# Graph and attention layer on one Trainium2 core: the clearing of a table's unused columns moved to a later stage, and half of a block's normalisation moved to ScalarE

## The chip, the cores and the metric

The kernel runs on one core of a Trainium2 chip. The metric is the device time of one execution in microseconds (us). The core has five engines that work side by side and wait for each other by semaphores: TensorE (PE, with its weight loads PEld), VectorE (DVE), ScalarE (ACT), GpSimd (POOL) and SyncE (SP). SP only issues DMA transfers in this kernel; POOL issues the indirect ones (gathers and scatters by a list of row numbers).

## The reference, cut to what matters

A graph layer and linear attention share a normalised input; a second graph layer (attention over edges) then mixes four experts.

```python
x: (12500, 256)   src, dst: (200000,), dst sorted
xn = layernorm(x)
h  = batchnorm(xn @ w1.T + b1); h = relu(h) @ w2.T + b2; xw = h @ w_gcn.T
gcn = segment_sum(xw[src] * norm[:, None], dst) + b_gcn        # self loops included
mix = linear_attention(xn)                                     # wq, wk, wv, wo
x = x + gcn + mix
hf = layernorm(x) @ W_gat; a_src, a_dst per head               # one row of 24 numbers per node
x = x + experts(layernorm(x), gates from attention over 131072 edges and self loops)
```

## The kernel before, in words

The 12,500 nodes are 25 blocks (NB) of 500, a block is four tiles (SUB) of 125 nodes. The stages follow one another, each a program block of its own:

- `first_half` (0 to 261 us): SP loads block k of x into one of three buffers (`load`, through `rows_in_two`, L163). DVE takes statistics (L615 to L620), ACT takes the root (L566), DVE inverts it (L625) and normalises the block's four tiles (L630). PE transposes (`turn`, L520), ACT copies the transposes out of PSUM (L592), PE multiplies by w1 (`project`, L530), ACT adds the bias (L603), DVE takes statistics of the result (L636). Beside it DVE counts the edge list's sections by `outside` (L643) and chooses rows (L649), POOL gathers these rows (L508) and ACT counts in them (`inside`, L574). SP stores the transposed block (L487).
- `table_rows` (271 to 400 us) writes the gather table to DRAM.
- `gather_mix` (400 to 2746 us): POOL gathers table rows, 128 rows of 1 KB in each of 1664 indirect DMAs, four to a group, in a ring of four groups (L1039). DVE builds a one-hot matrix for each group (L1377), PE multiplies (L1109), DVE adds the products to a sum that stays in SBUF (L1394). Other work is dealt out over the 832 slots of this loop (two gathers each): the attention, a sort of the second edge list and, from slot HIST = 547 on, the degrees of the second list. For the degrees SP loads that list once more (`raw_d`, L1097) and DVE waits for it in `numbers(0)`, slot 544 (L1472, L1473).
- `second_norm` fills the first 24 columns of the second table `gtab` (12,500 rows of 128 numbers, TWIDE; 24 used, TROW), whose other 104 columns have been cleared by one DMA from a zeroed tile: 12,500 pieces of 416 bytes. `gat_experts` gathers whole rows of `gtab`. Then `gat_finish` and `finale`.

Every engine runs its instructions in the order in which they are written. SP's DMAs all go through one hardware queue (q1 in the profile), POOL's through another (q0). In slot p of the gather loop PE runs `gathered(p)` and DVE `build` (even slots) and `add(p)`. Three limits tie them:

```python
pool.wait_ge(mm_s, 2 * (g - RING + 1))   # POOL, group g: the products of group g-4 are done
pe.wait_ge(add_s, 2 * p - 6)             # PE, slot p: the sums of slot p-4 are done
dve.wait_ge(raw_s, 16)                   # DVE, numbers(0): raw_d has landed
```

In `first_half` ACT's order for block k is: root(k+1), copies of block k, `inside(k-3)`, bias of block k. DVE's is: statistics(k+1), outside(k), inverse and normalise(k+1), choose(k), statistics of the product of block k-1.

Of the kernel before, what the change touches and what calls it, by code (L numbers as in the profile page):

```python
# [16 lines left out]
P = 128  # L17
# [368 lines left out]
def first_half(nc, K, A):  # L386
# [7 lines left out]
    with ExitStack() as ctx:  # L394
# [20 lines left out]
        st6 = m.sb("a_st6", [P, 2, SUB, 6])  # L415
        mv = m.sb("a_mv", [P, 2, SUB, 2])
        rs = m.sb("a_rs", [P, 2, SUB, 2])
        stats = m.sb("a_stats", [P, KC, NB, 6])
        node = m.sb("a_node", [P, NT])
        minus = m.sb("a_minus", [P, NT])  # L420
# [5 lines left out]
        diff = m.sb("a_diff", [P, 2, TN])  # L426
        deg = m.sb("a_deg", [P, NT])
        degree = m.sb("a_degree", [P, NT])
        blank = m.sb("a_blank", [P, TWIDE - TROW])
        tail = m.sb("tail", [P, 2], I32)  # L430
        after = m.sb("after", [P, 1], I32)
        fall = m.sb("fall", [P, 2])
# [3 lines left out]
        ph = m.ps("a_ph", [P, KC, 512])  # L436
        pw = m.ps("a_pw", [P, 512])
        pb = m.ps("a_pb", [P, 512])
        (w_s, both_s, bias_s, st_s, mv_s, eps_s, root_s, rec_s, xn_s, turned, xnT_s, h_s, hT_s, stat_s, deg_s, v,
         blank_s) = (m.sem("a_" + s) for s in (  # L440
             "w", "both", "bias", "st", "mv", "eps", "root", "rec", "xn", "turned", "xnT", "h", "hT", "stat", "deg", "v",
             "blank"))
        (dst_s, src_s, after_s, short_s, rows_out, pay_s, pairs_out, pad_s, edge_s, fell, spread_s, head_s, met_s, row_s, side_s,
         node_s, diff_s) = (m.sem("e_" + s) for s in (
             "dst", "src", "after", "short", "rows_out", "pay", "pairs_out", "pad", "edge", "fell", "spread", "head", "met", "row",
# [10 lines left out]
        with nc.Block() as block:  # L456
            @block.sync
            def _(sp):
                def load(k):
                    if k >= 3:  # L460
                        sp.wait_ge(xn_s, (k - 2) * SUB)
                    rows_in_two(sp, xin[:, k % 3], A.x[k * BN:(k + 1) * BN].rearrange("(j p) f -> p j f", p=TN), x_in[k % 3])

                by_part = A.dst.rearrange("(p c) -> p c", p=c)
                rows_in_two(sp, raw[:, 1], by_part, dst_s)
                load(0)
                for t, a in ((w1T, A.w1T), (w2, A.w2), (wgT, A.wgT)):
                    sp.dma_start(t[:], a.rearrange("(c p) o -> p c o", p=P)).then_inc(w_s, 16)
                with nc.allow_non_contiguous_dma(reason="biases"):
                    for t, a in ((b1c, A.b1), (b2c, A.b2)):  # L470
                        sp.dma_start(t[:], a.rearrange("(c p) -> p c", p=P)).then_inc(w_s, 16)
                with nc.allow_non_contiguous_dma(reason="one value per partition"):
                    sp.dma_start(after[0:c - 1], by_part[1:c, 0:1]).then_inc(after_s, 16)
                sp.wait_ge(short_s, 1)
                rows_in_two(sp, K.gcn_dst.rearrange("(p i) h -> p (i h)", p=c), short, rows_out)
                load(1)
                load(2)
                rows_in_two(sp, raw[:, 0], A.src.rearrange("(p c) -> p c", p=c), src_s)

                sp.wait_ge(blank_s, 1)  # L480
                sp.dma_start(K.gtab.rearrange("(t p) f -> p t f", p=TN)[:, :, TROW:TWIDE],
                             blank[q].unsqueeze(1).to_broadcast([TN, NT, TWIDE - TROW])).then_inc(blank_s, 16)
                for k in range(NB):
                    if k + 3 < NB:
                        load(k + 3)
                    sp.wait_ge(xnT_s, (k + 1) * KC)
                    sp.dma_start(K.xnT_d[k], xnT[:, k % 2]).then_inc(stored[k % 2], 16)  # L487
                    if k == 3:
                        sp.wait_ge(pay_s, 2)
                        rows_in_two(sp, K.gcn_pairs[0:E_GCN].rearrange("(p c) a -> p c a", p=c), K.gcn_pay, pairs_out)  # L490
                        sp.wait_ge(pad_s, 2)
                        sp.dma_start(K.gcn_pairs[E_GCN:E_GCN + P], tail[:]).then_inc(pairs_out, 16)
                for s in range(2):
                    sp.wait_ge(stored[s], 16 * ((NB + 1 - s) // 2))
                sp.wait_ge(blank_s, 17)
                sp.wait_ge(pairs_out, 48)

            @block.gpsimd
# [13 lines left out]
            @block.tensor  # L512
            def _(pe):
                def turn(k):
                    pe.wait_ge(xn_s, (k + 1) * SUB)
                    if k:
                        pe.wait_ge(xnT_s, k * KC)
                    for ch in range(KC):
                        for j in range(SUB):
                            mm = pe.transpose(ptr[:, ch, j * TN:(j + 1) * TN], xn[q, k % 2, j, ch * P:(ch + 1) * P],  # L520
                                              K.ident[q, q])
                        mm.then_inc(turned, 1)
# [39 lines left out]
            @block.scalar  # L562
            def _(act):
                def root(k):
                    act.wait_ge(eps_s, k + 1)
                    act.activation(rs[q, k % 2, :, 1], rs[q, k % 2, :, 0], ACT.Sqrt).then_inc(root_s, 1)  # L566

                def inside(g):
                    act.wait_ge(got[g % DEEP], 64 * (g // DEEP + 1))
                    if g:  # L570
                        act.wait_ge(side_s, 4 * g)
                    for j in range(4):
                        t = 4 * g + j
                        act.activation(seen[z, j], rows[z, g % DEEP, j], ACT.Sign, bias=minus[z, t:t + 1],  # L574
                                       accum_out=side[z, t:t + 1]).then_inc(side_s, 1)

                def paired(a):
                    act.wait_ge((src_s, dst_s)[a], 32)
                    act.copy(K.gcn_pay[0:c, :, a], raw[0:c, a]).then_inc(pay_s, 1)

                root(0)
                act.wait_ge(w_s, 16 * 5)
                act.wait_ge(node_s, 4)
                for k in range(NB):
                    if k + 1 < NB:
                        root(k + 1)
                    if k >= 2:
                        act.wait_ge(stored[k % 2], 16 * (k // 2))
                        act.wait_ge(h_s, (k - 1) * KC)
                    for ch in range(KC):  # L590
                        act.wait_ge(turned, k * KC + ch + 1)
                        act.copy(xnT[:, k % 2, ch], ptr[:, ch, 0:BN]).then_inc(xnT_s, 1)  # L592
                    if k in (1, 2):
                        paired(2 - k)
                    if k >= 3:
                        inside(k - 3)
                    if k == 20:
                        act.wait_ge(pay_s, 2)
                        act.wait_ge(edge_s, 7)
                        act.wait_ge(rows_out, 32)  # L600
                    for o in range(KC):
                        act.wait_ge(h_s, k * KC + o + 1)
                        act.activation(hT(k)[:, o], ph[:, o, 0:BN], ACT.Identity, bias=b1c[:, o:o + 1]).then_inc(hT_s, 1)  # L603
                for g in range(NB - 3, NB):
                    inside(g)
                act.wait_ge(deg_s, 1)
                act.activation(deg[q], deg[q], ACT.Sqrt).then_inc(root_s, 1)

            @block.vector
            def _(dve):  # L610
# [11 lines left out]
                def normalise(k):  # L622
                    s = k % 2
                    dve.wait_ge(root_s, k + 1)
                    dve.reciprocal(rs[q, s, :, 0], rs[q, s, :, 1]).then_inc(rec_s, 1)  # L625
                    dve.wait_ge(rec_s, k + 1)
                    if k >= 2:
                        dve.wait_ge(turned, (k - 1) * KC)
                    for j in range(SUB):
                        dve.tensor_scalar(xn[q, s, j], xin[q, k % 3, j], mv[q, s, j, 0:1], rs[q, s, j, 0:1],  # L630
                                          ALU.subtract, ALU.mult).then_inc(xn_s, 1)

# [34 lines left out]
                        dve.wait_ge(fell, 2)  # L667
                        dve.tensor_scalar(K.unsorted[:], pb[0:1, 0:1], 1.0, None, ALU.min).then_inc(edge_s, 1)

                dve.memset(blank[:], 0.0).then_inc(blank_s, 1)  # L670
                dve.tensor_scalar(node[:], K.iota[:, 0:NT], float(TN), K.part[:], ALU.mult, ALU.add).then_inc(node_s, 1)
                dve.tensor_tensor(diff[:, 0], K.ident[:, 1:POST], K.ident[:, 0:TN], ALU.subtract).then_inc(diff_s, 1)
                dve.wait_ge(node_s, 1)
# [252 lines left out]
def gather_mix(nc, K, A):  # L926
# [10 lines left out]
    with ExitStack() as ctx:  # L937
# [46 lines left out]
        heads = m.sb("m_heads", [P, KC, P])  # L984
        rn = m.sb("m_rn", [P, 2, SUB, 8])
        cnt2, upto, ends, tot = (m.sb("m_" + s, [P, NT]) for s in ("cnt2", "upto", "ends", "tot"))
        pa = m.ps("m_pa", [P, 512])
        pb = m.ps("m_pb", [P, 512])
        pc = m.ps("m_pc", [P, 512])
# [40 lines left out]
        with nc.Block() as block:  # L1030
# [14 lines left out]
            def _(sp):  # L1045
# [48 lines left out]
                        load2(k + 2)  # L1094
                for s in range(2):
                    sp.wait_ge(out_x[s], 32 * ((NB + 1 - s) // 2))
                sp.dma_start(raw_d, A.edge_index[1].rearrange("(p c) -> p c", p=P)).then_inc(raw_s, 16)  # L1097

            @block.tensor
            def _(pe):  # L1100
# [271 lines left out]
            def _(dve):  # L1372
# [241 lines left out]
                dve.tensor_scalar(bq[:, 1], bq[:, 0], -1.0, None, ALU.mult).then_inc(one_s, 1)  # L1614
                dve.tensor_tensor(b_out[0:1, 0], b_out[0:1, 0], b_out[0:1, 1], ALU.add).then_inc(one_s, 1)
                dve.memset(K.gat_last[:], 0).then_inc(one_s, 1)
                for p in range(SLOTS):
                    if p % 2 == 0:
                        tiles = tiles_of(p // 2)
# [932 lines left out]
```

## Time and profile before

| | us |
|---|---|
| median of 3 runs | 4793.2 (4790.67 to 4804.6) |
| the profiled execution | 4790.88 |
| its span in the trace | 4789.0 |
| PE busy | 3688.3 (77%) |
| POOL busy | 3085.5 (64%) |
| DVE busy | 2604.3 (54%) |
| ACT busy | 880.5 (18%) |

The shares are means over stages with different limits, so each stage is read for itself. The trace's times count from the start of the span. In a timeline a row is a start, a duration (of a whole run of equal instructions where xN stands at the end), an engine, a line of the kernel and the tiles; the bracket is the idle time of that engine before it and what ended it. SPq is the time that SP's issue of a DMA took, not that of its transfer. "issue" in the bracket is the engine's own time between instructions.

### The profile page before, as it was taken

Reading aid. Unit: us, or ns where it says so; the run is one execution under the profiler, and the core shown is the slowest. Engines: PE = TensorE matmul, PEld = TensorE weight load, DVE = VectorE, ACT = ScalarE, POOL = GpSimd, SP = SyncE. Lnnn points to the kernel's source line nnn. Section 1 sums busy time; section 2 is a strip of 40 time slices with the busy share of each in tenths; the row PEclk is TensorE's granted clock in tenths of the full one; section 3 lists DMA queues with packets and bytes.
Section 4 is the critical chain, followed back from the end, with each engine's and each line's share of the span. In section 5 each row is a group of like instructions: output and inputs, shape, how many; then the busy total and the mean of one; then the engine's idle time right before and its main releaser. Section 6 shows DMA issues by size and latency. Waiting matters only on the chain. (4 is left out here: it accounts for less than half of the span.)

```text
span 4789.0 us, 44151 instructions
## 1 busy us (share of the span) xinstructions
PE 3688.3 (77%) x13162; PEld 2442.9 (51%) x13162; DVE 2604.3 (54%) x6218; ACT 880.5 (18%) x1738; POOL 3085.5 (64%) x3019
## 2 busy tenths in 40 slices
PE   3667888888798998787887564799999999700377
PEld 1355555455555555555555354466666666500255
DVE  5946776666666556666666364134334333312476
ACT  2653222222100000000000011222222223200232
POOL 2515777777776776777777500777777777777630
PEclk7989999999887998777677655899999999955689
DMA  6645444444454664333333765444444334322588
GB/s 178 188 98 152 129 130 132 130 130 130 125 154 132 182 177 131 89 91 89 92 91 89 71 193 137 132 114 113 138 115 113 117 106 138 97 63 63 114 209 196
DMA packets 262492, 606.63 MB, mean 127 GB/s; under 512 B 88254, under 2 KB 144369, under 8 KB 256893
## 3 DMA queue, kind: packets, MB, share of 16 engines
q0 software_dynamic: 124496, 304.94, 24.1%
q1 hardware_dynamic: 137772, 299.02, 22.2%
q8 instruction: 103, 1.69, 0.1%
q14 instruction: 121, 0.99, 0.1%
HBM read 447.85 MB, written 155.88 MB: 126 GB/s over the span
## 5 line engine op out<-in xcount | busy, mean ns | idle before, releaser
L1039 POOL DMA_INDIRECT g_rows<-table,gcn_srcT x1664 | 1758.2, 1057 | 568.0 <-issue 485.7
L1109 PE MATMUL g_ps<-g_rows,g_hot 128*125 128x256 f32 x3328 | 1064.3, 456 | 337.4 <-issue 229.6
L1902 POOL DMA_INDIRECT n_rows<-gtab,so_own x1122 | 1095.6, 977 | 341.9 <-issue 341.9
L1394 DVE TENSOR_TENSOR acc<-acc,g_ps 125x256 f32 x1664 | 696.4, 419 | 691.6 <-PE g_ps L1109 565.6
L1109 PEld LDWEIGHTS g_ps<-g_rows,g_hot 128*125 128x125 f32 x3328 | 685.8, 223 | 622.8 <-issue 410.0
L1842 PE MATMUL p_ph<-f_xfT,f_w 128*128 128x500 f32 x1344 | 576.7, 585 | 64.2 <-DMA f_xfT<-xfT_d 64.2
L1848 PE MATMUL p_py<-f_w,f_hh 128*125 128x256 f32 x2688 | 590.4, 379 | 0.0
L1848 PEld LDWEIGHTS p_py<-f_w,f_hh 128*125 128x125 f32 x2688 | 504.5, 188 | 101.1 <-issue 27.4
L2045 DVE TENSOR_TENSOR p_ob<-p_py,p_xb 125x512 f32<-125x512 f32 x168 | 115.6, 691 | 699.0 <-PE p_py L1848 698.6
L1842 PEld LDWEIGHTS p_ph<-f_xfT,f_w 128*128 128x128 f32 x1344 | 256.4, 191 | 348.6 <-issue 343.5
L2073 ACT ACTIVATE f_hh<-p_ph,f_b 128x500 f32<-128x500 f32 x336 | 221.4, 677 | 616.4 <-PE p_ph L1842 616.1
L1377 DVE TENSOR_TENSOR g_hot<-iota,gcn_dstT 128x500 f32<-128x500 f32 x416 | 281.2, 676 | 27.6 <-issue 16.9
L1199 PE MATMUL m_pa<-m_area 128*100 128x125 bf16 x1024 | 276.5, 405 | 0.0
L2125 PE MATMUL f_pt<-ident,gat_tail 128*20 128x128 f32 x3 | 0.8, 402 | 285.1 <-PEq L84 285.1
L1199 PEld LDWEIGHTS m_pa<-m_area 128*100 128x100 bf16 x1024 | 170.5, 167 | 86.1 <-issue 29.8
L1129 PE MATMUL m_pb<-m_area 128*125 128x512 f32 x400 | 197.4, 616 | 19.0 <-DVE m_area L1404 18.8
L508 POOL DMA_INDIRECT so_x<-gcn_dst,a_row x100 | 100.6, 1006 | 147.2 <-DVE a_row L649 124.0
L530 PE MATMUL a_ph<-a_xnT,w1T 128*128 128x500 f32 x200 | 105.8, 679 | 102.1 <-ACT a_xnT L592 102.1
L1895 POOL DMA_INDIRECT n_first<-gtab,gat_head x1 | 0.9, 943 | 278.1 <-POOLq L84 278.1
L1842 PE MATMUL z_ph<-f_xfT,f_w 128*128 128x500 f32 x256 | 118.2, 619 | 67.6 <-ACT f_hh L2321 54.2
L1790 ACT ACT_TABLE_LOAD x1 | 1.3, 1283 | 881.0 <-PEq L84 881.0
L2125 PEld LDWEIGHTS f_pt<-ident,gat_tail 128*20 128x20 f32 x3 | 0.3, 107 | 285.6 <-issue 285.5
(338 smaller groups left out, 4329.8 us busy)
## 6 DMA issues: line engine op xcount, KB each, us to landing
o_d<-p_ob SPq DMA_DIRECT2D x21, 1920.0 KB
z_ob<-o_d SPq DMA_DIRECT2D x21, 1920.0 KB
g_rows<-table,gcn_srcT POOLq DMA_INDIRECT x1664, 3.0
n_rows<-gtab,so_own POOLq DMA_INDIRECT x1122
gout<-n_o SPq DMA_DIRECT2D x33, 408.0 KB, 2.5
xnT_d<-a_xnT SPq DMA_DIRECT2D x25, 500.0 KB
m_area<-xnT_d SPq DMA_DIRECT2D x25, 500.0 KB, 3.8
qT_d<-m_area SPq DMA_DIRECT2D x25, 500.0 KB, 3.1
```

The costliest lines, as they stand in the source:

```text
L530: mm = pe.matmul(ph[:, o, 0:BN], w1T[:, ch, o * P:(o + 1) * P], xnT[:, k % 2, ch], start=ch == 0, stop=ch == KC - 1)
L1039: pool.indirect_dma_start(out=rows[:, g % RING, j], out_offset=None, in_=K.table, in_offset=bass.IndirectOffsetOnAxis(ap=K.gcn_srcT[:, 4 * ...
L1109: mm = pe.matmul(ps[q, p % 4, b], hot[:, g % 4, 2 * j + b], rows[:, g % RING, 2 * j + b], start=True, stop=True, skip_group_check=True)
L1129: pe.matmul(pb[q], xnT[:, k % 2, c, j * TN:(j + 1) * TN], wkv[:, c].rearrange("p a o -> p (a o)"), start=c == 0, stop=False, skip_group_ch ...
L1199: mm = pe.matmul(pa[0:NT, q], ot[:, r % 2, b], on[:, r % 2, :, b], start=r == 0 and b == 0, stop=r == half - 1 and b == HB - 1)
L1377: dve.tensor_tensor(hot[:, g % 4], K.iota[:, q].unsqueeze(1).to_broadcast(shape), K.gcn_dstT[:, 4 * g:4 * g + 4].unsqueeze(2).to_broadcast ...
L1394: dve.tensor_tensor(a, a, ps[q, p % 4, b], ALU.add).then_inc(add_s, 1)
L1842: mm = pe.matmul(ph[:, o, 0:BN], self.w1[:, e, c, o * P:(o + 1) * P], self.xfT[:, s, c], start=c == 0, stop=c == KC - 1)
L1848: mm = pe.matmul(py[0:TN, e % 2, j // 2, (j % 2) * D:(j % 2 + 1) * D], self.hh[:, e % 2, c, j * TN:(j + 1) * TN], self.w2[:, e, c], start= ...
L1902: pool.indirect_dma_start(out=rows[:, c % 3, j], out_offset=None, in_=K.gtab, in_offset=bass.IndirectOffsetOnAxis(ap=K.gat_src[:, c * W + ...
L2045: dve.tensor_tensor(ob[0:TN, s, pair, e], py[0:TN, e % 2, a].rearrange("p (j f) -> p j f", j=2), xb[0:TN, pair], ALU.add).then_inc(ob_s, 1)
L2073: act.activation(X.hh[:, e % 2, o], ph[:, o, 0:BN], ACT.Gelu, bias=X.b1[:, e, o:o + 1]).then_inc(hh_s, 1)
```

## The change

1. The 104 unused columns of `gtab` are no longer cleared in `first_half`. The zeroed tile, its semaphore, the memset and the DMA move to `gather_mix`. There the DMA is issued by SP after the last stores of the attention's result, directly ahead of the load of `raw_d`.
2. In `first_half` DVE normalises two of a block's four tiles, ACT the other two, as `rs * x + off`. DVE computes `off = -mean * rs` in one more small instruction. ACT's part stands right behind root(k+1), ahead of the copies of block k. SP's reload of a buffer and PE's transposes wait for both halves.

```diff
-                sp.wait_ge(blank_s, 1)
-                sp.dma_start(K.gtab.rearrange("(t p) f -> p t f", p=TN)[:, :, TROW:TWIDE],
-                             blank[q].unsqueeze(1).to_broadcast([TN, NT, TWIDE - TROW])).then_inc(blank_s, 16)
                 for k in range(NB):
                     if k + 3 < NB:
                         load(k + 3)
...
+                def normalise(k):
+                    s = k % 2
+                    act.wait_ge(off_s, k + 1)
+                    if k >= 2:
+                        act.wait_ge(turned, (k - 1) * KC)
+                    for j in range(SUB // 2, SUB):
+                        act.activation(xn[q, s, j], xin[q, k % 3, j], ACT.Identity, bias=off[q, s, j:j + 1],
+                                       scale=rs[q, s, j, 0:1]).then_inc(xna_s, 1)
...
                     if k + 1 < NB:
                         root(k + 1)
+                        normalise(k + 1)
...
                     dve.wait_ge(rec_s, k + 1)
+                    dve.scalar_tensor_tensor(off[q, s], mv[q, s, :, 0], -1.0, rs[q, s, :, 0], ALU.mult, ALU.mult
+                                             ).then_inc(off_s, 1)
                     if k >= 2:
                         dve.wait_ge(turned, (k - 1) * KC)
-                    for j in range(SUB):
+                    for j in range(SUB // 2):
...
                 for s in range(2):
                     sp.wait_ge(out_x[s], 32 * ((NB + 1 - s) // 2))
+                sp.wait_ge(blank_s, 1)
+                sp.dma_start(K.gtab.rearrange("(t p) f -> p t f", p=TN)[:, :, TROW:TWIDE],
+                             blank[q].unsqueeze(1).to_broadcast([TN, NT, TWIDE - TROW])).then_inc(blank_s, 16)
                 sp.dma_start(raw_d, A.edge_index[1].rearrange("(p c) -> p c", p=P)).then_inc(raw_s, 16)
+                sp.wait_ge(blank_s, 17)
```

SP's order of DMAs at the start of `first_half`, before (`a_xin` is a buffer for x; the load behind the clearing is that of block 3; `acc<-in_src` is the source list):

```order
L163 DMA acc<-in_src 120x1600
L163 DMA acc<-in_src 5x1600
L481 DMA gtab<-a_blank 125x100x104
L163 DMA a_xin<-in_x 120x4x256
L163 DMA a_xin<-in_x 5x4x256
L487 DMA xnT_d<-a_xnT 128x1000
```

In the change the row of L481 is gone from here, and block 3's load follows the source list. SP's order at the end of its work in `gather_mix`, now (`m_area<-in_edge_index` is the load of `raw_d`; before, it followed the stores of `pre_d` directly):

```order
L163 DMA pre_d<-m_area 120x1024
L163 DMA pre_d<-m_area 5x1024
L1108 DMA gtab<-m_blank 125x100x104
L1110 DMA m_area<-in_edge_index 128x1024
L1040 UNCONDITIONAL_BRANCH
```

The clearing now stands between the last stores and the load that DVE waits for. ACT's order for one block in `first_half`, now (`a_rs` root, `a_xn` normalise, `a_xnT` copies, `so_own` inside, `acc` bias):

```order
L562 ACTIVATE a_rs<-a_rs 125x4
L570 ACTIVATE a_xn<-a_xin,a_off,a_rs 125x256 x2
L599 COPY a_xnT<-a_ptr 128x500 x2
L579 ACTIVATE so_own,a_side<-so_x,a_minus 126x400 x4
L610 ACTIVATE acc<-a_ph,b1c 128x500 x2
```

The row of L570 is new; the other four stood in this order before.

## Rows read from the trace of the kernel before

**Rows 1.** Timeline of SP, first stage: start, duration of the issue, DMA.

```profile
15.20 0.34 SPq L481 DMA_DIRECT2D gtab<-a_blank  x1
16.38 60.49 SPq L163 DMA_DIRECT2D a_xin<-in_x  x2
```

**Rows 2.** Timeline of DVE around its longest wait in the first stage.

```profile
35.76 0.16 DVE L663 TENSOR_TENSOR fall<-fall 128x1 f32<-128x1 f32 x1
81.09 1.40 DVE L615 BATCH_NORM_STATS2 a_st<-a_xin 125x6 f32<-125x256 f32 x4 [45.17 <-DMA a_xin<-in_x]
```

**Rows 3.** Windows: busy PE, PEld, DVE, ACT, POOL; last PE clock, DMA share, GB/s.

```profile
30.00:40.00 10.00, 4.48 (x16) 2.36 (x16) 5.78 (x15) 3.19 (x4) 5.21 (x6) 0.91 0.53 148
50.00:60.00 10.00, 0.00 (x0) 0.00 (x0) 0.00 (x0) 0.00 (x0) 0.00 (x0) 0.50 0.38 98
```

**Rows 4.** Timeline of the first blocks: DVE's second and third inverse, PE's first product.

```profile
22.03 6.49 PE L530 MATMUL a_ph<-a_xnT,w1T 128*128 128x500 f32 x8 [3.70 <-ACT a_xnT L592]
...
23.16 0.18 DVE L625 RECIPROCAL a_rs<-a_rs 125x4 f32<-125x4 f32 x1
...
31.04 0.17 DVE L625 RECIPROCAL a_rs<-a_rs 125x4 f32<-125x4 f32 x1
```

**Rows 5.** Timeline of one later block of the first stage, DVE, ACT and PE.

```profile
132.30 1.39 DVE L615 BATCH_NORM_STATS2 a_st<-a_xin 125x6 f32<-125x256 f32 x4
...
134.47 1.03 ACT L592 COPY a_xnT<-a_ptr 128x500 f32<-128x500 f32 x2
...
135.56 3.62 PE L530 MATMUL a_ph<-a_xnT,w1T 128*128 128x500 f32 x8 [2.84 <-ACT a_xnT L592]
...
136.88 0.16 DVE L625 RECIPROCAL a_rs<-a_rs 125x4 f32<-125x4 f32 x1
...
137.07 1.38 DVE L630 TENSOR_SCALAR a_xn<-a_xin,a_mv,a_rs 125x256 f32<-125x256 f32 x4
...
139.22 0.68 ACT L603 ACTIVATE acc<-a_ph,b1c 128x500 f32<-128x500 f32 x1 [0.70 <-PE a_ph L530]
139.62 1.39 DVE L615 BATCH_NORM_STATS2 a_st<-a_xin 125x6 f32<-125x256 f32 x4
...
141.67 0.21 ACT L566 ACTIVATE a_rs<-a_rs 125x4 f32<-125x4 f32 x1 [1.78 <-DVE a_rs L620]
```

**Rows 6.** Groups by line and form: busy us, mean ns of one.

```profile
L630 DVE TENSOR_SCALAR a_xn<-a_xin,a_mv,a_rs 125x256 f32<-125x256 f32 x100 | 34.5, 409 | 0.9
L835 ACT ACTIVATE acc<-r_tmp,dinv 125x256 f32<-125x256 f32 x100 | 44.7, 497 | 33.2 <-DVE r_tmp L911 33.2
L828 ACT ACTIVATE r_r<-acc,r_shift,r_scale 128x500 f32<-128x500 f32 x50 | 37.0, 789 | 3.4 <-DVE r_shift L854 3.4
```

**Rows 7.** PE: first and last of six long products, the next; a window inside.

```profile
98.94 5.32 PE L530 MATMUL a_ph<-a_xnT,w1T 128*128 128x500 f32 x8 [2.25 <-ACT a_xnT L592]
...
208.67 5.31 PE L530 MATMUL a_ph<-a_xnT,w1T 128*128 128x500 f32 x8 [2.84 <-ACT a_xnT L592]
...
215.99 3.62 PE L530 MATMUL a_ph<-a_xnT,w1T 128*128 128x500 f32 x8 [1.14 <-ACT a_xnT L592]
...
208.00:211.00 3.00, 2.33 (x3) 1.11 (x4) 2.96 (x12) 3.00 (x10) 1.24 (x2) 0.63 0.67 237
```

**Rows 8.** The load of raw_d: SP's timeline, and issue to landing by line.

```profile
1887.25 0.36 SPq L1097 DMA_DIRECT2D m_area<-in_edge_index  x1
DMA to landing us min/median/max: 4.0/4.0/4.0
```

**Rows 9.** DVE's timeline at slot 544; POOL's group of gathers up to 1894.0 us.

```profile
1895.91 0.90 DVE L1473 TENSOR_SCALAR m_area<-m_area 128x1024 int32<-128x1024 int32 x1
L1039 POOL DMA_INDIRECT g_rows<-table,gcn_srcT x1096 | 1111.1, 1014 | 390.2 <-issue 317.2 <-PE g_ps L1109 72.9
```

**Rows 10.** POOL's waits from 1895 to 2660 us: us in total, times, longest.

```profile
POOL g_rows L1039 <- PE g_ps L1109: 3.4, 11, 0.3
```

**Rows 11.** Window of the gather loop shortly before the load, columns as in rows 3.

```profile
1860.00:1880.00 20.00, 18.28 (x80) 11.83 (x79) 11.55 (x26) 0.56 (x1) 15.26 (x16) 1.00 0.43 131
```

More of the change, by code:

```diff
@@ L417, in first_half @@
         rs = m.sb("a_rs", [P, 2, SUB, 2])
+        off = m.sb("a_off", [P, 2, SUB])
         stats = m.sb("a_stats", [P, KC, NB, 6])
@@ L428, in first_half @@
         degree = m.sb("a_degree", [P, NT])
-        blank = m.sb("a_blank", [P, TWIDE - TROW])
         tail = m.sb("tail", [P, 2], I32)
@@ L438, in first_half @@
         pb = m.ps("a_pb", [P, 512])
[L439 to L442, printed above, removed]
+        (w_s, both_s, bias_s, off_s, xna_s, st_s, mv_s, eps_s, root_s, rec_s, xn_s, turned, xnT_s, h_s, hT_s, stat_s, deg_s, v) = (m.sem("a_" + s) for s in (
+             "w", "both", "bias", "off", "xna", "st", "mv", "eps", "root", "rec", "xn", "turned", "xnT", "h", "hT", "stat", "deg", "v"))
         (dst_s, src_s, after_s, short_s, rows_out, pay_s, pairs_out, pad_s, edge_s, fell, spread_s, head_s, met_s, row_s, side_s,
@@ L460, in load @@
                     if k >= 3:
-                        sp.wait_ge(xn_s, (k - 2) * SUB)
+                        sp.wait_ge(xn_s, (k - 2) * (SUB // 2))
+                        sp.wait_ge(xna_s, (k - 2) * (SUB // 2))
                     rows_in_two(sp, xin[:, k % 3], A.x[k * BN:(k + 1) * BN].rearrange("(j p) f -> p j f", p=TN), x_in[k % 3])
@@ L494, in _ @@
                     sp.wait_ge(stored[s], 16 * ((NB + 1 - s) // 2))
-                sp.wait_ge(blank_s, 17)
                 sp.wait_ge(pairs_out, 48)
@@ L514, in turn @@
                 def turn(k):
-                    pe.wait_ge(xn_s, (k + 1) * SUB)
+                    pe.wait_ge(xn_s, (k + 1) * (SUB // 2))
+                    pe.wait_ge(xna_s, (k + 1) * (SUB // 2))
                     if k:
@@ L581, in _ @@
                 root(0)
+                normalise(0)
                 act.wait_ge(w_s, 16 * 5)
@@ L668, in check_order @@
                         dve.tensor_scalar(K.unsorted[:], pb[0:1, 0:1], 1.0, None, ALU.min).then_inc(edge_s, 1)
-                dve.memset(blank[:], 0.0).then_inc(blank_s, 1)
                 dve.tensor_scalar(node[:], K.iota[:, 0:NT], float(TN), K.part[:], ALU.mult, ALU.add).then_inc(node_s, 1)
@@ L986, in gather_mix @@
         cnt2, upto, ends, tot = (m.sb("m_" + s, [P, NT]) for s in ("cnt2", "upto", "ends", "tot"))
+        blank = m.sb("m_blank", [P, TWIDE - TROW])
+        blank_s = m.sem("m_blank_s")
         pa = m.ps("m_pa", [P, 512])
@@ L1616, in _ @@
                 dve.memset(K.gat_last[:], 0).then_inc(one_s, 1)
+                dve.memset(blank[:], 0.0).then_inc(blank_s, 1)
                 for p in range(SLOTS):
```

## The prediction

> **What bounds the kernel now.** The chain that ended last says little here, because its part of the span lies in the closing stages; the change sits in two earlier ones, so I read each stage by its timeline and its waits.
>
> In the first stage two things bound the time. The first is one long hole: DVE finishes at 35.9 us and stands still until block 3 of x lands at 81.09 us, 45.2 us in all [rows 2]. The reason is in SP's rows: the clearing is issued at 15.20 us, and the two transfers behind it, block 3's, need 60.5 us only to be issued, until 76.9 us [rows 1]. While every engine stands still the DMA engines move a steady 98 GB/s at a busy share of 0.38 [rows 3], and that can only be the clearing. Its 12,500 pieces of 416 bytes are 5.2 MB, which at 98 GB/s is 53 us. So the clearing blocks SP's queue for as long as it drains; it is not the DMA engines that are full. After the hole DVE is the bound: in a typical block it starts its statistics at 132.30 and again at 139.62 us, a period of 7.32 us, with no idle time to speak of between, while PE and ACT wait [rows 5].
>
> In the gather stage POOL is the bound: between 1895 and 2660 us it waits for PE for 3.4 us in all [rows 10], and issues a gather every 1.25 us (16 in 20 us [rows 11]). So a delay of POOL there is a delay of the end.
>
> **Part 1: the clearing leaves the first stage.** Block 3's load then stands behind the source list, which SP had issued by 15.2 us, and the 45.2 us go [rows 2]. What is late next is the second block's root. ACT now normalises before it copies, so block 0's copies wait for `off` of block 1, which DVE has behind its second inverse, at about 23.5 us [rows 4]. With two normalisations (1.1 us, below) and the copies (1.03 [rows 5]) PE's first product begins at 25.7 instead of 22.03, and takes 6.49 us at the low clock [rows 4]. Its last bias (0.68) and the next root (0.21) end near 33.0 us, so DVE's third inverse comes at 33.0 instead of 31.04 [rows 4]. That gives 2.0 us back: **-43.2 us** (ends: -45.2, if the late root finds DVE busy elsewhere, and -42).
>
> **Part 2: the split normalisation.** DVE drops two of four tiles: four take 1.38 us with 0.41 for one [rows 5, 6], so 0.33 us from start to start, 0.65 us for two. `off` on 4 columns costs about 0.08 in a pipelined row. DVE alone would need 7.32 - 0.65 + 0.08 = 6.75 us.
>
> But a new circle closes through ACT and PE, because the copies now wait for `off`. I count it from the start of `off`: 0.20 until ACT sees it. ACT's normalisation has two per-partition operands; the trace has 0.50 us for 256 columns with one and 0.79 for 500 columns with two [rows 6], so I take 0.60, a second one starting 0.51 after the first; the copies begin at 1.22 and end at 2.25 (1.03 [rows 5]). PE starts at 2.31 and needs 3.62 [rows 5]: 5.93. The second bias starts at 5.97, the root 0.58 behind it, and ends at 6.76 (0.21 [rows 5]). DVE's inverse (0.16) and `off` again: 7.0 us. So the block takes 7.0, not 6.75: 21 blocks behind the start gain 0.32 each, 6.7 us.
>
> The price is PE's clock. Six of the 20 products between 98 and 240 us took 5.1 to 5.3 us instead of 3.62; over three us in one of them the mean granted clock was 0.63 of full speed, a mixture of the two levels 1.2 and 2.4 GHz [rows 7]. Before, DVE hid this: the next product simply waited 1.14 instead of 2.84 us [rows 7]. On the new circle each costs 1.7 us. PE's pause shrinks from 2.84 to about 2.4 us; the six long products followed pauses of 2.25 to 2.9 us [rows 7], so I take half as many, three: 5.1 us. Net **-2 us**; ends: -12 (DVE alone) and +6 (seven or eight long products).
>
> The Trainium skill, "TensorE: Matmul & The Clock Gate", section "HAM oscillation", tells of a kernel whose bursts each start at the low clock again because each waits for its data. By that rule the product would be long in all blocks; the rows show six of 20, so far against it. It is the third rival below.
>
> **Part 3: the clearing arrives in the gather stage.** SP issued `raw_d` at 1887.25 us, it landed 4.0 us later [rows 8], and DVE used it at 1895.9 us [rows 9]: 4.6 us to spare. Now the clearing is issued at that moment and `raw_d` behind it on the same queue, as block 3 was. I take 53 us of draining, 1.7 to begin (an estimate), and 3 because gathers run beside it: between 30 and 40 us six gathers of 126 rows of 800 bytes (0.6 MB, 60 GB/s) ran too, and of 148 GB/s [rows 3] about 88 were left for the clearing. So it ends at 1945 and `raw_d` lands at 1949. DVE waits 53 us in slot 544, and behind the wait stand all one-hot matrices and sums of later slots.
>
> POOL feels it after its ring: 1096 gathers are out at 1894 us, 274 groups [rows 9]. With the sum of slot 544 done, PE may go on to slot 548 and POOL to group 277: 16 more gathers of 1.25 us, to 1914.1 us. It starts again when DVE has `raw_d`, has done its first conversion (0.9 [rows 9]) and the sum of slot 545 (1.0), and PE slot 549 (about 1.4): 1952.3 us. That is 38.2 us, and the next groups come about 1.5 late while DVE catches up: **+40 us**. POOL has no slack later [rows 10] to win it back. Ends: +32, if the clearing drains in 53 us from its issue and `raw_d` lands with its end; +47, if it holds the queue for the 61.7 us from 15.20 to 76.9 us [rows 1] and DVE needs 4 us more; nearest is the first stage's own rate.
>
> The gathers beside it already move 131 GB/s with other traffic [rows 11]. The Trainium skill, "DMA: Bandwidth & Descriptors", section "Queues, rings and completion order", says that a DMA engine takes its queues in turn, packet by packet. By that the clearing would run at half rate for the 25 us of gathers, 12 us longer, and the sum would end 10 us later; the 88 of 98 GB/s in [rows 3] speak against a half.
>
> The memset (0.15 us) only changes its stage, and SP's last wait hides under the 800 us of gathers that follow.
>
> **Sum.** -43.2 - 2 + 40 = -5 us against the profiled execution's 4790.9 (2.3 us below the median of the runs): **4786 us**. A measurement of this kernel can tell about 0.3% from no change, 14.4 us, so this is no change. With the ends of the parts it could be 4766 (-45.2 - 12 + 32) to 4802 (-42 + 6 + 47), both ends unlikely together; this case's own range is 4774 to 4798.
>
> **The rivals.**
> - *`raw_d` is not held up*, since it uses DMA engines that the clearing leaves free (share 0.38 [rows 3]). Then nothing is lost in the gather stage: 4790.9 - 45 = 4746 us, faster. Against it: block 3's load met the same engines and waited 60.5 us [rows 1]. Chance 0.10.
> - *The hole was not the clearing's*, but the load or its issue is late for another reason. Then the first stage keeps its hole and the gather stage still pays: 4790.9 - 2 + 40 = 4829 us, slower. Against it: DMA traffic of 98 GB/s with nothing else under way [rows 3]. Chance 0.03.
> - *PE's low clock sits on the new circle in every block.* Place: the product of the first stage, which now holds up root, inverse and `off`. Price: 1.7 us in each of 21 blocks, less the 6.7 gained: +29 us, and 4790.9 - 43 + 29 + 40 = 4817 us, slower. It decides from about 15 long products on (-43 + 40 - 6.7 + 15 x 1.7 = +16). For it: pauses of 2.3 us already brought a long product. Against it: behind a long product the next was never long. Chance 0.07.
>
> **How the numbers follow.** The forecast case has 0.80: 0.08 of it faster than 4776.5, 0.68 within 0.3%, 0.04 slower than 4805.3. With 0.10 of the first rival and 0.03 for faster cases not thought of, taken from the middle, faster is 0.21; slower is 0.04 + 0.03 + 0.07 = 0.14; same is 0.65. The range of 4770 to 4808 holds the forecast's case and the milder part of the third rival (up to about 12 long products) and leaves out the first and the second.
>
> **What would show it.** Right: no wait of DVE above a few us near 36 us, the first stage 40 to 50 us shorter; in the gather stage, a DVE wait of 45 to 60 us ahead of the conversion of `raw_d`, and a POOL wait for PE of 35 to 45 us. In the first stage blocks of about 7.0 us, with ACT's normalisation waiting for DVE's `off` and PE for ACT's copies. Wrong: `raw_d` landing within 10 us of its issue; blocks still at 7.3 us or above 7.6; a POOL wait below 30 us.

## The result, and the profile after

The changed kernel takes 4816.9 us in the median against 4794.06 us for the kernel before: ratio 1.0049 (95% interval 1.0037 to 1.0062), 0.5% slower. Forecast were 4786 us, no change, and a range of 4770 to 4808. One of its 20 executions, of 5101.1 us, was in a slower state of the chip and is left out of the ratio. Its profiled execution took 4818.74 us with a span of 4816.6 us.

| stage (from the trace's rows) | before | after | difference | forecast |
|---|---|---|---|---|
| first stage, until DVE starts on `r_bn` | 270.9 | 247.7 | -23.2 | -45.2 |
| from there to POOL's last gather of `gather_mix` | 2446.8 | 2500.4 | +53.6 | +40 |
| from there to the end of the span | 2071.3 | 2068.5 | -2.8 | 0 |
| span | 4789.0 | 4816.6 | +27.6 | -5 |

Two of the three parts went as forecast. DVE's timeline in the first stage of the changed kernel:

```profile
23.05 0.17 DVE L632 RECIPROCAL a_rs<-a_rs 125x4 f32<-125x4 f32 x1
...
33.04 0.18 DVE L632 RECIPROCAL a_rs<-a_rs 125x4 f32<-125x4 f32 x1 [2.60 <-ACT a_rs L562]
...
37.50 1.41 DVE L622 BATCH_NORM_STATS2 a_st<-a_xin 125x6 f32<-125x256 f32 x4
```

Block 3's statistics begin at 37.50 us without a wait, where they stood until 81.09 [rows 2]. The third inverse comes at 33.04 us, after a wait for the late root: 33.0 was forecast.

The other end of the move, as SP's timeline, then DVE's and POOL's, in the gather stage of the changed kernel:

```profile
1877.34 0.27 SPq L1108 DMA_DIRECT2D gtab<-m_blank  x1
1877.65 57.86 SPq L1110 DMA_DIRECT2D m_area<-in_edge_index  x1
```

```profile
1939.66 0.69 DVE L1487 TENSOR_SCALAR m_area<-m_area 128x1024 int32<-128x1024 int32 x1 [50.96 <-DMA m_area<-in_edge_index]
```

```profile
1943.88 0.94 POOL L1049 DMA_INDIRECT g_rows<-table,gcn_srcT  x1 [40.21 <-PE g_ps L1123]
1950.37 0.94 POOL L1049 DMA_INDIRECT g_rows<-table,gcn_srcT  x1 [1.81 <-PE g_ps L1123]
1957.64 0.94 POOL L1049 DMA_INDIRECT g_rows<-table,gcn_srcT  x1 [1.69 <-PE g_ps L1123]
```

The load of `raw_d` needs 57.9 us only to be issued, as block 3's load did [rows 1]; DVE waits 51 us (53 forecast) and POOL 40.2, then 1.8 and 1.7 (38.2 and 1.5 forecast).

The third part did not. PE in the first stage, with the pause and its releaser in the bracket:

```profile
75.54 5.32 PE L526 MATMUL a_ph<-a_xnT,w1T 128*128 128x500 f32 x8 [3.97 <-ACT a_xnT L599]
...
84.19 3.62 PE L526 MATMUL a_ph<-a_xnT,w1T 128*128 128x500 f32 x8 [2.47 <-ACT a_xnT L599]
...
105.05 3.62 PE L526 MATMUL a_ph<-a_xnT,w1T 128*128 128x500 f32 x8 [2.48 <-ACT a_xnT L599]
108.51 1.02 PE L516 MATMUL a_ptr<-ident,a_xn 125*128 125x125 f32 x8
112.00 3.62 PE L526 MATMUL a_ph<-a_xnT,w1T 128*128 128x500 f32 x8 [2.47 <-ACT a_xnT L599]
115.46 1.02 PE L516 MATMUL a_ptr<-ident,a_xn 125*128 125x125 f32 x8
118.95 5.32 PE L526 MATMUL a_ph<-a_xnT,w1T 128*128 128x500 f32 x8 [2.47 <-ACT a_xnT L599]
124.10 1.02 PE L516 MATMUL a_ptr<-ident,a_xn 125*128 125x125 f32 x8
127.60 5.10 PE L526 MATMUL a_ph<-a_xnT,w1T 128*128 128x500 f32 x8 [2.48 <-ACT a_xnT L599]
...
212.95 5.09 PE L526 MATMUL a_ph<-a_xnT,w1T 128*128 128x500 f32 x8 [2.48 <-ACT a_xnT L599]
```

From 84 to 118 us the blocks follow each other in 6.95 us (105.05 to 112.00), as forecast (7.0). The product at 118.95 us is long, and from there on every one is but that of the last block: the last of the series starts at 212.95, twelve in a row, and a block takes 8.4 to 8.7 us. Four products ahead of 84 us are long too; behind the one at 75.54 us the pause was 2.47 us, and the next product, at 84.19, was short. The windows view of the changed kernel tells the clock (columns: window, length, busy PE, PEld, DVE, ACT, POOL, PE clock, DMA share, GB/s):

```profile
80.00:118.00 38.00, 24.10 (x91) 12.78 (x89) 35.56 (x126) 30.97 (x80) 21.14 (x22) 1.00 0.66 193
120.00:220.00 100.00, 71.91 (x192) 35.51 (x191) 77.65 (x275) 69.10 (x176) 46.98 (x48) 0.80 0.51 155
```

The granted clock is full from 80 to 118 us and 0.80 from 120 on, a mixture of 2.4 and 1.2 GHz. DVE, which set the pace before [rows 5], is busy for 78 of these last 100 us. The timeline of one long block, all engines, shows what a long product holds up:

```profile
124.30 0.68 ACT L610 ACTIVATE acc<-a_ph,b1c 128x500 f32<-128x500 f32 x1 [2.30 <-PE a_ph L526]
...
124.88 0.20 ACT L562 ACTIVATE a_rs<-a_rs 125x4 f32<-125x4 f32 x1
125.11 0.18 DVE L632 RECIPROCAL a_rs<-a_rs 125x4 f32<-125x4 f32 x1 [1.73 <-ACT a_rs L562]
125.33 0.16 DVE L634 SCALAR_TENSOR_TENSOR a_off<-a_mv,a_rs 125x4 f32<-125x4 f32 x1
...
125.52 1.09 ACT L570 ACTIVATE a_xn<-a_xin,a_off,a_rs 125x256 f32<-125x256 f32 x2 [0.44 <-DVE a_off L634]
...
126.52 1.03 ACT L599 COPY a_xnT<-a_ptr 128x500 f32<-128x500 f32 x2
...
127.60 1.20 PE L526 MATMUL a_ph<-a_xnT,w1T 128*128 128x500 f32 x1 [2.48 <-ACT a_xnT L599]
```

Read downwards this is the circle of the prediction: product, bias, root, inverse, `off`, ACT's normalisation, copies, next product. Each step starts when the one before is done, so a product that is 1.7 us longer moves the whole block. What the circle leaves PE is a pause of 2.48 us, however long the product ahead of it was. Before, the pause behind a long product was only 1.14 us [rows 7], because DVE's pace did not change. The timeline doesn't show why the next product is long again.

### The profile page after: what moved, and what is told of

It is laid out like the page before. It is cut to its first block and busy times, and to the rows that moved or that the text cites. A ratio compares the mean times of both kernels' runs of the same rounds, so it can differ in the third digit from the quotient of the medians.

```text
span 4816.6 us, 44201 instructions
## 1 busy us (share of the span) xinstructions
PE 3707.8 (77%) x13162; PEld 2452.5 (51%) x13162; DVE 2592.9 (54%) x6193; ACT 906.1 (19%) x1788; POOL 3087.5 (64%) x3019
## 5 line engine op out<-in xcount | busy, mean ns | idle before, releaser
L526 PE MATMUL a_ph<-a_xnT,w1T 128*128 128x500 f32 x200 | 117.3, 742 | 67.1 <-ACT a_xnT L599 67.1
```

Of the source, the lines that this page charges most:

```text
L526: mm = pe.matmul(ph[:, o, 0:BN], w1T[:, ch, o * P:(o + 1) * P], xnT[:, k % 2, ch], start=ch == 0, stop=ch == KC - 1)
```

## The experiments

Three readings were to be told apart. Theory C: the missing 20 us are PE's clock on the new circle. Rival S: the longer chain through ScalarE costs, whatever the clock. Rival G: the split did as forecast, and the clearing takes more from the gathers than the wait shows. Ratios are to the kernel before on the same chip, with 95% intervals; as the kernels ran on more than one chip, rows are compared by their ratios. "Long" counts those of the 25 products that take 5.0 us or more, "in a row" those of them that directly follow another long one.

| kernel | median, us | ratio | first stage ends | long (in a row) | POOL's longest wait for PE |
|---|---|---|---|---|---|
| before | 4794.06 | 1 | 270.9 | 8 (0) | 9.7 |
| the change | 4816.9 | 1.0049 (1.0037 to 1.0062) | 247.7 | 16 (13) | 40.2 |
| e1 move only | 4783.22 | 0.9988 (0.9975 to 1.0) | 228.6 | 9 (0) | 40.4 |
| e2 split only | 4815.91 | 1.0042 (1.0025 to 1.0059) | 298.4 | 18 (14) | 11.0 |
| e3 raw_d first | 4777.52 | 0.9967 (0.9955 to 0.998) | 253.1 | 19 (16) | 8.1 |
| e4 filled pauses | 4783.48 | 0.9979 (0.9965 to 0.9993) | 229.7 | 3 (0) | 40.4 |
| e6 move, raw_d first | 4747.79 | 0.9891 (0.9871 to 0.9912) | 228.0 | 11 (0) | 9.1 |
| e7 copies first | 4734.47 | 0.9865 (0.9843 to 0.9887) | 215.1 | 6 (0) | 7.5 |
| e8 copies first, filled | 4739.13 | 0.9879 (0.9856 to 0.9902) | 215.1 | 1 (0) | 8.1 |

**e1, the move alone.** From the change, whose `off`, ACT function `normalise` and waits for it go too:

```diff
                 root(0)
-                normalise(0)
...
                         root(k + 1)
-                        normalise(k + 1)
...
-                    for j in range(SUB // 2):
+                    for j in range(SUB):
```

> The change without its second half: the clearing stands in the gather stage, ahead of raw_d, as in the change; VectorE normalises all four tiles again. Theory C (TensorE's clock on the new circle cost the missing 20 us): the first stage ends about 45 us earlier than before the change (226 instead of 270.9 us), its blocks take about 7.3 us, the gather pays 40 to 45 us; 4787 to 4795 us, ratio 0.998 to 1.000. Rival G (the split did as forecast, and the gather stage pays more than the wait for raw_d, because the clearing slows its transfers): the gather pays 55 to 65 us, 4803 to 4813 us. Rival S (the split's longer chain through ScalarE costs, whatever the clock): same as C here.

The first stage ends at 228.6 us (C and S: 226), DVE waits 51.1 us for `raw_d`, and the ratio is within C's, though the median is 4 us below C's range. Moving the clearing alone is no loss; G's 4803 to 4813 us fall.

**e2, the split alone.** The clearing back in the first stage (its lines in the gather stage go):

```diff
+                sp.wait_ge(blank_s, 1)
+                sp.dma_start(K.gtab.rearrange("(t p) f -> p t f", p=TN)[:, :, TROW:TWIDE],
+                             blank[q].unsqueeze(1).to_broadcast([TN, NT, TWIDE - TROW])).then_inc(blank_s, 16)
                 for k in range(NB):
```

> The change's second half alone: the clearing is back in the first stage, ScalarE normalises two of four tiles. Theory C and rival S: blocks behind the hole take 7.0 to 8.6 us instead of 7.3, most of the products over 5 us; first stage 15 to 25 us longer; 4809 to 4819 us, ratio 1.003 to 1.005. Rival G: blocks of 7.0 us with few long products, 4787 to 4795 us.

4815.91 us and 18 long products: the split by itself brings the loss. The first stage is 27.5 us longer than before, a little over the 15 to 25 expected. Here the series begins at 144.18 us and lasts until 263.62; its first rows in PE's timeline:

```profile
144.18 5.32 PE L532 MATMUL a_ph<-a_xnT,w1T 128*128 128x500 f32 x8 [2.47 <-ACT a_xnT L605]
...
152.83 5.08 PE L532 MATMUL a_ph<-a_xnT,w1T 128*128 128x500 f32 x8 [2.48 <-ACT a_xnT L605]
```

**e3, `raw_d` ahead of the clearing.**

```diff
+                sp.dma_start(raw_d, A.edge_index[1].rearrange("(p c) -> p c", p=P)).then_inc(raw_s, 16)
                 sp.wait_ge(blank_s, 1)
                 sp.dma_start(K.gtab.rearrange("(t p) f -> p t f", p=TN)[:, :, TROW:TWIDE],
                              blank[q].unsqueeze(1).to_broadcast([TN, NT, TWIDE - TROW])).then_inc(blank_s, 16)
-                sp.dma_start(raw_d, A.edge_index[1].rearrange("(p c) -> p c", p=P)).then_inc(raw_s, 16)
```

> The changed kernel with two lines exchanged: raw_d is loaded first and the clearing is issued behind it. Theory C: the waits of 51 us (VectorE) and 40 us (POOL) go, nothing else; 40 us faster than the change: 4774 to 4780 us. Rival G: the clearing still costs the gather 10 to 20 us by its traffic: 4787 to 4797 us.

The wait of DVE is gone, POOL's longest is 8.1 us, and 39 us of 4816.9 go. So part 3 is the wait alone: the clearing's own traffic beside the gathers costs nothing beyond the interval of the ratio, 12 us wide, and G's 4787 to 4797 us fall. The series of long products is still there (19).

**e4, the pauses filled.** The changed kernel, whose waits all stay:

```diff
                     turn(k)
...
+                    if k:
+                        for _ in range(8):
+                            pe.matmul(pw[:, 0:P], K.ones[:], K.ones[:], start=True, stop=True, skip_group_check=True)
                     project(k)
```

> The changed kernel, with eight products of 128 x 128 ones (whose sums nobody reads) put into TensorE's pause of 2.5 us in each block, between the turns and the product. Theory C: with TensorE busy there the clock stays high, every product takes about 3.6 us and the block 6.95 us; the first stage ends 18 to 24 us earlier than in the change, at about 226 us; 4793 to 4800 us. Rival S: the products' length is not what the block waits for; the first stage stays at 247 us or gets longer, because TensorE has more to do: 4815 to 4830 us.

This is the experiment that decides between C and S. PE's timeline, and a window, of e4:

```profile
98.75 3.62 PE L526 MATMUL a_ph<-a_xnT,w1T 128*128 128x500 f32 x8 [0.68 <-ACT a_xnT L602]
102.21 1.02 PE L516 MATMUL a_ptr<-ident,a_xn 125*128 125x125 f32 x8
103.06 1.95 PE L539 MATMUL a_pw<-ones 128*128 128x128 f32 x16
105.70 3.62 PE L526 MATMUL a_ph<-a_xnT,w1T 128*128 128x500 f32 x8 [0.69 <-ACT a_xnT L602]
```

```profile
120.00:200.00 80.00, 72.48 (x365) 47.93 (x364) 78.00 (x273) 66.78 (x175) 45.38 (x46) 1.00 0.64 193
```

PE has 1.95 us more to do in every block, and the first stage is 18 us shorter. From 84.85 us to the end of the blocks no product is long, and a block takes 6.95 us (98.75 to 105.70); the granted clock is 1.00. For the series C is shown and S falls: the same chain with the clock high makes no loss there. The median is 33 us under the change's, and under C's 4793 to 4800; 15 of the 33 us lie outside the first stage, and what they are stays open. It equals e1's (4783.5 and 4783.2), and the first stages end within 1.1 us of each other: in this order the split gains nothing even with the clock held. Its blocks are shorter than e1's (6.95 against 7.3 us), but its eighth product begins at 84.85 us, where e1's begins at 75.56.

**e6, the best of the move.** e1 with the two DMAs exchanged as in e3.

> The kernel before with the clearing in the gather stage, behind raw_d; VectorE normalises all four tiles. First stage as in e1 (ends at about 228 us), no wait for raw_d: 42 us faster than before, 40 faster than e1: 4742 to 4752 us, ratio 0.990. If e1's gain over the forecast sum came from somewhere else than the hole, it stays above 4760 us.

As expected: with both waits gone, part 1 is worth 1.1%.

**e7, ScalarE's normalisation off the circle.** e3 with one call moved:

```diff
                     if k + 1 < NB:
                         root(k + 1)
-                        normalise(k + 1)
...
                         act.copy(xnT[:, k % 2, ch], ptr[:, ch, 0:BN]).then_inc(xnT_s, 1)
+                    if k + 1 < NB:
+                        normalise(k + 1)
```

> e3 (clearing behind raw_d, split normalisation) with ScalarE's two normalisations behind its copies instead of ahead of them. Theory C with its circle: the copies no longer wait for off, TensorE's pause shrinks by some 1.4 us, a long product is hidden beside VectorE's 6.75 us unless several follow each other; blocks of 6.75 to 7.2 us, first stage ends at 215 to 225 us instead of 253; 4735 to 4748 us, 30 to 40 us faster than e3. Rival S' (the split itself brings the low clock, wherever ScalarE normalises, and long products hold the block up): blocks above 8 us, 4770 us or more.

The first stage is 38.0 us shorter than e3's (253.1 to 215.1), and the ratio falls from 0.9967 to 0.9865, some 49 us (33 to 66 by the ends of the two intervals) where 30 to 40 were expected. PE's timeline around a long product and in a later block:

```profile
52.13 5.32 PE L526 MATMUL a_ph<-a_xnT,w1T 128*128 128x500 f32 x8 [2.06 <-ACT a_xnT L598]
...
59.27 3.62 PE L526 MATMUL a_ph<-a_xnT,w1T 128*128 128x500 f32 x8 [0.79 <-ACT a_xnT L598]
...
126.10 3.62 PE L526 MATMUL a_ph<-a_xnT,w1T 128*128 128x500 f32 x8 [2.24 <-ACT a_xnT L598]
...
132.83 3.62 PE L526 MATMUL a_ph<-a_xnT,w1T 128*128 128x500 f32 x8 [2.25 <-ACT a_xnT L598]
```

The block takes 6.73 us (126.10 to 132.83), DVE's own 6.75 of the prediction. Behind a long product the pause shrinks to 0.79 us and the next product is short again: none of the six follows another. So rival S' falls: the split alone does not bring the series, ACT's place in the order does. And the split, in this order, is worth 12.9 us of the first stage against e6 (228.0 to 215.1). This version beats both kernels: the one before by 1.35%, the change by 1.8% (0.9865 over 1.0049).

**e8, e7 with filled pauses** (the edit of e4).

> e7 with the eight products of ones in each pause of TensorE, as in e4. If VectorE alone bounds e7's blocks: the same time as e7, within 5 us. If long products still cost in e7: 5 to 15 us faster than e7.

The first stages end within 0.1 us of each other, with one long product instead of six. Where DVE sets the pace, the six long products cost nothing that shows; of these kernels filling helped only on the circle.

**e9, e10, e11: why the clearing takes 53 us.** The changed kernel each time, `raw_d` behind the clearing, and the clearing written otherwise: over 16 partitions, in two halves of the columns, in whole rows.

The lines that issue it, of e9, of e10 and of e11 (the two lines taken away are the same for all; `SIXT` is 12,496, `CLEAR_W` 52):

```diff
+                sp.dma_start(K.gtab[0:SIXT].rearrange("(p t) f -> p t f", p=16)[:, :, TROW:TWIDE],
+                             blank[0:16].unsqueeze(1).to_broadcast([16, SIXT // 16, TWIDE - TROW])).then_inc(blank_s, 16)
+                sp.dma_start(K.gtab[SIXT:N, TROW:TWIDE], blank[0:N - SIXT]).then_inc(blank_s, 16)
-                sp.dma_start(K.gtab.rearrange("(t p) f -> p t f", p=TN)[:, :, TROW:TWIDE],
-                             blank[q].unsqueeze(1).to_broadcast([TN, NT, TWIDE - TROW])).then_inc(blank_s, 16)
```

```diff
+                for a in (TROW, TROW + CLEAR_W):
+                    sp.dma_start(K.gtab.rearrange("(t p) f -> p t f", p=TN)[:, :, a:a + CLEAR_W],
+                                 blank[q, 0:CLEAR_W].unsqueeze(1).to_broadcast([TN, NT, CLEAR_W])).then_inc(blank_s, 16)
```

```diff
+                sp.dma_start(K.gtab.rearrange("(p a r) f -> p a (r f)", p=TN, r=2),
+                             blank[q].unsqueeze(1).to_broadcast([TN, NT // 2, 2 * TWIDE])).then_inc(blank_s, 16)
```

> The changed kernel with the same clearing, at the same place ahead of raw_d, written as 16 runs of 781 rows (and 4 rows more) instead of 100 x 125. Theory D (the clearing drains at 98 GB/s because few DMA engines carry it): the DMA share rises, the clearing drains in 15 to 25 us, VectorE's wait for raw_d falls from 51 to 12 to 25 us and POOL's longest from 40 to under 10; 30 to 40 us faster than the change: 4777 to 4787 us. Rival Q (each small piece costs the queue its time, whatever engine takes it): 98 GB/s and the wait of 51 us stay; 4810 to 4820 us.

> The changed kernel with the clearing as two transfers of half the columns each: the same 5.2 MB, in 25,000 pieces of 208 bytes instead of 12,500 of 416. Rival Q (each piece costs the queue about 4.2 ns): it drains at about 50 GB/s in 106 us, VectorE waits about 104 us for raw_d, POOL some 90; 50 us slower than the change: 4862 to 4875 us. Theory Y (the queue moves some 98 GB/s whatever the pieces): wait and time as in the change, 4810 to 4822 us.

> The changed kernel with whole rows cleared, two at a time: 6.4 MB instead of 5.2, in 6,250 pieces of 1024 bytes (the first 24 columns of each row are cleared too; a later stage writes them). Rival Q: 6,250 pieces of 4.2 ns drain in 26 us, VectorE waits 20 to 30 us, POOL 10 to 17; 23 to 30 us faster than the change: 4787 to 4794 us. Theory Y: 6.4 MB at 98 GB/s are 65 us, VectorE waits about 63 us; 12 us slower than the change: 4825 to 4833 us.

In windows where every engine stands still (DMA share and GB/s at the end of the row), one fence for each of e9, e10 and e11:

```profile
1910.00:1920.00 10.00, 0.00 (x0) 0.00 (x0) 0.00 (x0) 0.00 (x0) 0.00 (x0) 0.50 0.65 91
```

```profile
1902.00:1915.00 13.00, 0.00 (x0) 0.00 (x0) 0.00 (x0) 0.00 (x0) 0.00 (x0) 0.50 0.44 49
1925.00:1950.00 25.00, 0.00 (x0) 0.00 (x0) 0.00 (x0) 0.00 (x0) 0.00 (x0) 0.50 0.39 80
```

```profile
1896.00:1912.00 16.00, 0.00 (x0) 0.00 (x0) 0.00 (x0) 0.00 (x0) 0.00 (x0) 0.50 0.34 121
```

DVE's use of `raw_d`, in the same order:

```profile
1930.30 0.69 DVE L1489 TENSOR_SCALAR m_area<-m_area 128x1024 int32<-128x1024 int32 x1 [44.20 <-DMA m_area<-in_edge_index]
```

```profile
1957.41 0.69 DVE L1489 TENSOR_SCALAR m_area<-m_area 128x1024 int32<-128x1024 int32 x1 [82.24 <-DMA m_area<-in_edge_index]
```

```profile
1920.80 0.69 DVE L1487 TENSOR_SCALAR m_area<-m_area 128x1024 int32<-128x1024 int32 x1 [53.95 <-DMA m_area<-in_edge_index]
```

Times: e9 4810.91 us (ratio 1.0034, 1.0013 to 1.0056), e10 4837.97 (1.0112, 1.0075 to 1.015), e11 4820.14 (1.0057, 1.0037 to 1.0076). From the issue of the clearing (1866.74, 1864.54 and 1857.15 us) to these rows it is 63.6, 92.9 and 63.7 us, against 62.3 in the change (1877.34 to 1939.66). D falls: the DMA share is 0.65 instead of 0.38 [rows 3], and nothing is faster (91 GB/s against 98); the wait itself is 7 us shorter only because DVE came later after the issue. The time is as Q expected for e9. In e10 and e11 Q and Y both miss. In e10 the first half drains at 49 GB/s and the second, as many pieces of the same size, at 80, so that the wait lies between Y's 51 and Q's 104 us. Its median holds 9 us of a longer first stage besides: the series of long products is in all three kernels (18, 23 and 18 long, 15, 21 and 14 in a row). In e11 half as many pieces drain at 121 GB/s, and the wait of 54 us lies between Q's 20 to 30 and Y's 63. What holds the clearing at about 53 us stays open; at what byte a piece begins and ends differs between the halves of e10, but that was not tried by itself.

## Why the prediction was wrong

- **What bounds the kernel** held: the hole is the clearing's, and POOL pays in the gather stage for what DVE waits.
- **Part 1** held in its main term: e1's first stage is 42.3 us shorter, in the change block 3's statistics begin within 0.4 us of the forecast start (37.50 us against 35.9 and 2.0), and the third inverse comes at 33.04. But e1 has nothing of ACT's new place, and the 2.0 us given back for it were too few: the change's eighth product begins at 84.19 us, 8.6 later than e1's, behind four long products, two of which also began late (after pauses of 3.11 and 3.97 us).
- **Part 3** held: 40 us by POOL's wait and 39 by e3's median. From the clearing's issue to DVE's use of `raw_d` it was 62.3 us, where 61.7 to its landing were forecast; no row shows the 1.7 us to begin by itself. The +53.6 us of the one pair of profiles is not more cost: of six profiles without the wait (before, e2, e3, e6, e7, e8) this stretch lasts 2440.9 to 2463.8 us, mean 2448.3, and of five with it (the change, e1, e4, e9, e11) 2475.8 to 2500.4, mean 2488.8: 40.5 us. It scatters by 23 to 25 us from one execution to another, so stage sums of single profiles can't be trusted to less. The medians can: by the ends of the two intervals e4 is 21 to 46 us under the change, so that its first stage's 18 us don't cover it.
- **Part 2** failed, in the sentence "I take half as many, three". The circle, its 7.0 us and the 1.7 us for each long product were right (6.95 measured, 5.32 less 3.62). But the change's profile has 12 in one series and 16 in all, so the first stage won 23 us instead of 45. Of these 22 us about 13 are the series (e4, without it, ends its first stage 18.0 us earlier, and 5.1 had been allowed for); the other 9 lie in the blocks ahead of it. The split's net was not -2 but about +20. The +22.8 us of the medians against -5 forecast are 28 more; 22 are the first stage's, and the other 6 are within the interval of the ratio. The count was taken from a kernel in which PE did *not* sit on the circle. There a long product shortens the pause behind it (1.14 us [rows 7]), and the next is short: none follows another in before, e1, e6 and e7. On the circle the pause is about 2.48 us behind a long product too, and long ones follow each other in each of the six kernels that have it unfilled, 13 to 21 times (the change, e2, e3, e9, e10, e11). The prediction had the row, and used it the wrong way round: "behind a long product the next was never long" was put against the third rival, but it was read where the pause could shrink, and the change takes that away. A pause that can't shrink is not enough by itself: behind the long products at 44.55 and 75.54 us of the change it was 2.48 and 2.47 us, and the next was short.
- **The third rival**, with 0.07 and 4817 us, is what came. That the time fits to 0.1 us is luck: the rival counted 21 long products and +29 us, where 16 came and the net was about +20. "In every block" is not exact: five blocks from 84 us on had the same pause of 2.48 us and a short product. The Trainium skill, "TensorE: Matmul & The Clock Gate", section "HAM oscillation", tells of bursts that each begin cold because each waits for its data; for the blocks from 118.95 us on the trace agrees, for the five before it does not.
- **The first two rivals** fell: `raw_d` was held up for 57.9 us, and the hole went.

What starts a series is open, and so is why the long products ahead of it did not go on: it began at 118.95 us in the change, 98.63 in e3 and 144.18 in e2.

## What to carry to other kernels

Before a step is put between two others on an in-order engine, ask whether it closes a circle: here the copies, ready at once, were placed behind a step that waits for a round trip, and moving that one call behind them turned the split's loss into a gain (first stages of 253.1 and 215.1 us in e3 and e7, against 228.0 without the split). A count of slow events taken from a trace in which they were hidden is no forecast for a kernel in which they are not: ask what made the next one fast again, and whether the change takes that away. A large transfer of small pieces belongs behind the loads that somebody waits for on its queue, wherever it stands.

## What the runs showed that was not expected

- PE's low clock came in series: with the pause fixed by a chain of other engines, in each of the six kernels that have the circle and its pauses unfilled a series of 12 to 22 long products lasted until the last block but one (12 in the change, 15 from 98.63 us on in e3); with 1.95 us of idle work in each pause none began.
- The clearing's drain follows neither its bytes nor its pieces: 5.2 MB at 98 GB/s in pieces of 416 bytes, the halves of 208 bytes at 49 and at 80 GB/s, 6.4 MB in pieces of 1024 bytes at 121 GB/s. The Trainium skill, "DMA: Bandwidth & Descriptors", section "Why a DMA increments its semaphore by 16 and not by 1", says that a transfer is spread over as many engines as the largest number up to 16 that divides the outermost dimension on both of its sides. By that 125 gives 5 and 16 gives 16; the shares of 0.38 [rows 3] and 0.65 agree in direction, but the rate does not follow them.
